# Two chained transformer layers on one core: the 16-bit turns move from TensorE to transposing transfers, and two copies move from ScalarE to VectorE

## The chip, the cores and the metric

The kernel runs on one core of a Trainium2 chip. A core has five engines that work side by side: TensorE (PE in the profile, with PEld for its weight loads), VectorE (DVE), ScalarE (ACT), GpSimd (POOL) and SyncE (SP), which here only issues transfers. Each runs its own list of instructions in order and waits on semaphores for the others; transfers are carried by 16 DMA engines. The metric is the time of one execution on the device in microseconds (us); less is better.

## The reference, cut to what matters

Two layers, each attention followed by a feed-forward part, over 2048 rows (2 batches of 1024) of 256 numbers. In the kernel the rows are 16 tiles of 128, numbered n = 0 to 15.

```python
# layer 0: x is (2, 1024, 256); 32 heads of 8, 8 key heads; causal
q, k, v = x @ Wq + bq, x @ Wk + bk, x @ Wv + bv      # then rotary on q and k
attn = softmax(where(kpos > qpos, -inf, q k^T / sqrt(8))) ; out = (attn @ v) @ Wo + bo
# feed-forward, operands cast to fp8
act = gelu(x8 @ w_gating[0]) * (x8 @ w_gating[1]) ; y = act8 @ w_linear
# layer 1: at each row, 16 heads of 16 attend to each other within the row
q, k = rope(x @ wq.T), rope(x @ wk.T) ; v = x @ wv.T
attn = softmax(einsum('bshd,bstd->bsht', q, k) / 4) @ v ; out = attn @ wo.T
# feed-forward with ternary weights: silu-gated hidden of 1024, RMS norm, projection to 256
```

The terms around these (layer norms, residual sums) are in both kernels alike.

## The kernel before

Every engine has a list of steps in ORDER, written out as words such as `qk.37`: the stage and its number. Each stage is a small function that waits on semaphores and issues its instructions; the list alone sets the order on an engine. A second pass exists for inputs out of range and is not run here. For layer 0 the score blocks ("quads", 144 in all, `qk`, `exp`, `mask`, `pv`) are the long thread through the lists; the other stages are strewn between them, several tiles ahead or behind.

TensorE wants its operand with the inner dimension on the partitions, so activations have to be turned (transposed) before a product. Four turns matter here:

- **Keys and queries of layer 0.** `qh` (ACT), `q0`, `kl` (DVE) and `ql` (POOL) write rows of fp16 pairs, high part and rest, into QX. `qxT` (PE, L639) turns them, 2 blocks of 128x128 for the keys and 8 for the queries of a tile, into PSUM; `kTc` (L1228) and `qTc` (L1235) on DVE copy them to kT and qT, which `qk` (L685) reads.
- **Normalized rows of layer 1.** `xn1` (DVE, f32) is turned by `xn1T` (PE, L590 and L591, f32), and `xn1Tc` (DVE, L1369 and L1371) makes the fp16 high part and the rest out of PSUM into xhs, for `qkv1` and `gu`.
- **Hidden activations of layer 1.** `ssq` (ACT, L1032) sums squares of the 1024 hidden values, `ssm` (DVE) and `rsg` (POOL) make the factor, `hxa` (ACT, L1037) writes the high part and `hx` (DVE, L1482) the rest, both fp16, into hx_b, of which there is one. `hxT` (PE, L876) turns 2 x 8 blocks, `hTc` (DVE, L1491) copies them to hT (one, too), and `dn1` (PE, L885) multiplies.
- **Queries and keys within a row (f32).** `gT` turns them on PE; `gTq` (DVE, L1422) and `gTk` (ACT, L1007) copy them out.

Results of PE other than scores and the attention sum go to three PSUM banks psA, psB and psC, which all fills share in the order of the list: a fill waits until the fill three before it has been emptied (EMPTIED). SP's list issues the transfers, in order: loads, the round trip of layer 1 through DRAM (`vw`, `vr` with three gathers L522, `ow`, `at1r`) and the output.

Of the kernel before, what the change touches and what calls it, by code (L numbers as in the profile page):

```python
# [1782 lines left out]
```

## Time and profile before

| what | value |
|---|---|
| three runs, median (least to most) | 600.06 us (599.37 to 602.33) |
| span of the profiled execution | 601.7 us |
| TensorE busy | 562.0 us, 93% |
| ScalarE busy | 469.6 us, 78% |
| VectorE busy | 426.6 us, 71% |
| GpSimd busy | 233.6 us, 39% |
| mean granted TensorE clock | 0.983 of full speed |

The span runs from the first to the last instruction of the one execution that was profiled; it is the only time of that execution that there is, and it is 0.3% above the median of the three runs. Busy time is the union of an engine's instructions. An engine that is nearly always busy in a stretch sets that stretch's length; one that is idle half of it can take more work there for nothing, if the work comes at the right moment.

### The profile page before, as it was taken

The numbers are of one execution on the slowest core, as the hardware profiler recorded it, in microseconds if no ns is written. First come the engines' busy times: TensorE is split into PE (matmuls) and PEld (weight loads), VectorE is DVE, ScalarE is ACT, GpSimd is POOL, SyncE is SP. The second block draws the span as 40 slices with busy tenths as digits, with TensorE's granted clock in tenths as the row PEclk, the third lists the DMA queues.
The fourth block names the chain that finished last, engine by engine and source line by source line (L and its number), as shares of the span: only waits on it lengthen the run. The fifth ranks groups of instructions, "written<-read, shape, count | busy, mean of one in ns | idle before, by whom it ended". The sixth has DMA issues, their size and how long they took to land. (4 is left out here: it accounts for less than half of the span.)

```text
span 601.7 us, 13300 instructions
## 1 busy us (share of the span) xinstructions
PE 562.0 (93%) x5153; PEld 290.7 (48%) x5153; DVE 426.6 (71%) x909; ACT 469.6 (78%) x607; POOL 233.6 (39%) x302
## 2 busy tenths in 40 slices
PE   3687898999999999999999999999999999999976
PEld 1332434433555555645544555565445454456654
DVE  5658889988789558856699877565555365658765
ACT  2378899999988997999878898777979877972631
POOL 3748666043533163306855641360232150250100
PEclk9778999999999999999999999999999999999989
DMA  8810101102041223030110330531301304035632
GB/s 265 303 36 2 36 1 35 36 2 49 6 62 33 33 59 39 27 37 3 19 17 2 64 54 27 89 55 27 54 10 36 45 20 69 17 68 85 94 57 48
DMA packets 150914, 30.40 MB, mean 51 GB/s; under 512 B 133952, under 2 KB 149568, under 8 KB 150848
## 3 DMA queue, kind: packets, MB, share of 16 engines
q1 hardware_dynamic: 150272, 29.19, 24.4%
q8 instruction: 42, 0.69, 0.5%
q10 hardware_dynamic: 576, 0.33, 0.3%
q14 instruction: 24, 0.20, 0.1%
HBM read 19.02 MB, written 10.49 MB: 49 GB/s over the span
## 5 line engine op out<-in xcount | busy, mean ns | idle before, releaser
L958 ACT ACTIVATE Pt<-psS 128x1024 f32<-128x1024 f32 x288 | 281.7, 1047 | 44.8 <-PE psS L685 25.9
L699 PE MATMUL psV<-Pt,vaug 128*32 128x512 f32 x1152 | 150.3, 611 | 0.3 <-POOL Pt L1645 0.3
L1645 POOL TENSOR_SCALAR_AFFINE_SELECT Pt<-Pt 128x1024 f32<-128x1024 f32 x64 | 71.7, 1145 | 43.8 <-ACT Pt L958 43.8
L685 PE MATMUL psS<-qTf,kTf 32*128 32x512 f16 x576 | 74.9, 390 | 7.3 <-ACT Pt L958 3.7
L685 PEld LDWEIGHTS psS<-qTf,kTf 32*128 32x128 f16 x576 | 20.3, 91 | 82.9 <-ACT Pt L958 48.1
L1695 POOL TENSOR_TENSOR ss<-ss,mhalf 128x1 f32<-128x1 f32 x16 | 9.5, 596 | 111.3 <-DVE ss L1476 111.3
L699 PEld LDWEIGHTS psV<-Pt,vaug 128*32 128x32 f32 x1152 | 25.7, 109 | 41.9 <-issue 35.9
L1016 ACT ACTIVATE stage<-psS 128x1024 f32<-128x1024 f32 x32 | 31.0, 1020 | 8.1 <-PE psS L821 7.9
L1686 POOL TENSOR_TENSOR r<-qk,cos 128x256 f32<-128x256 f32 x16 | 11.9, 744 | 63.9 <-ACT qk L991 58.0
L866 PE MATMUL psB<-wguT,xhs 128*128 128x512 bf16 x108 | 27.8, 380 | 0.0
L1032 ACT ACTIVATE qtmp<-qtmp 128x1024 bf16<-128x1024 f32 x16 | 16.9, 1059 | 12.9 <-PE psA L876 8.4
L1318 DVE SCALAR_TENSOR_TENSOR gw<-gw,gb 128x512 f32<-128x512 f32 x32 | 24.9, 781 | 2.5 <-ACT gw L973 2.5
L1327 DVE SCALAR_TENSOR_TENSOR ga<-gw,gb 128x512 bf16<-128x512 f32 x32 | 23.6, 738 | 3.9 <-ACT gw L984 3.8
L1636 POOL TENSOR_TENSOR QXf<-rt,QXf 128x512 f16<-128x512 f32 x16 | 19.1, 1195 | 18.1 <-ACT QXf L945 18.1
L1608 POOL TENSOR_SCALAR rs<-mv 128x1 f32<-128x1 f32 x16 | 5.3, 329 | 49.6 <-DVE mv L1164 49.6
L1625 POOL TENSOR_TENSOR rt<-qkv,cs 128x320 f32<-128x320 f32 x16 | 14.7, 916 | 24.5 <-DVE QXf L1220 15.8
L984 ACT ACTIVATE gw<-gw 128x512 f32<-128x512 f32 x32 | 21.2, 661 | 3.0 <-DVE gw L1318 2.9
L1482 DVE SCALAR_TENSOR_TENSOR qtmp<-qtmp,ss 128x1024 f16<-128x1024 f32 x16 | 21.4, 1336 | 2.9 <-ACT qtmp L1037 2.9
L866 PE MATMUL psC<-wguT,xhs 128*128 128x512 bf16 x88 | 22.8, 382 | 0.0
L973 ACT ACTIVATE gw<-gb 128x512 f32<-128x512 bf16 x32 | 21.2, 670 | 0.1
L885 PE MATMUL psA<-wpT,stmp 128*128 128x256 bf16 x176 | 21.1, 273 | 0.0
L1628 POOL TENSOR_TENSOR rt<-qkv,sn 128x160 f32<-128x160 f32 x32 | 20.9, 673 | 0.0
(381 smaller groups left out, 1246.5 us busy)
## 6 DMA issues: line engine op xcount, KB each, us to landing
qkvscr<-rqkv SPq DMA_DIRECT2D x16, 384.0 KB, 2.5
G<-qkvscr SPq DMA_DIRECT2D x24, 128.0 KB, 3.7
stage<-in_wg SPq DMA_DIRECT2D x4, 512.0 KB, 8.8
w8g<-qkvscr SPq DMA_DIRECT2D x16, 128.0 KB, 3.8
oscr<-o SPq DMA_DIRECT2D x16, 128.0 KB, 3.3
at<-oscr SPq DMA_DIRECT2D x16, 128.0 KB, 2.0
out<-yout SPq DMA_DIRECT2D x16, 128.0 KB, 2.5
x<-in_x SPq DMA_DIRECT2D x1, 1536.0 KB, 12.2
```

Of the source, the lines that this page charges most:

```text
L685: e.matmul(psS[j], kd[32 * j:32 * j + k, h, 128 * at:128 * at + 128], qd[32 * j:32 * j + k, 4 * h:4 * h + 4, :].rearrange("p s n -> p (s n ...
L699: ins = e.matmul(psV[32 * j:32 * j + 32, :], vaug[:, at, j, 32 * h:32 * h + 32], Pt[(4 * Q + j) % NP], start=(kb == 0 and h == 0), stop=(k ...
L866: ins = e.matmul(bank[:], src[:, pt, 128 * c:128 * c + 128], wguT[:, c, c0:c0 + 512], start=(k == 0), stop=(k == 3))
L885: ins = e.matmul(bank[:, 0:256], hT[:, pt, s, :], wpT[:, s, :], start=(k == 0), stop=(k == 15))
L958: e.activation(flat(Pt4[:, u % NP:u % NP + 2, :]), flat(psS4[:, j:j + 2, :]), ACT.Exp, scale=scale).then_inc(S["exp"], 1)
L973: e.activation(gw[:, half, :], gb[:, half, :], ACT.Square).then_inc(S["sq"], 1)
L984: e.activation(gw[:, half, :], gw[:, half, :], ACT.Tanh, scale=GC * GA).then_inc(S["th"], 1)
L1016: e.activation(P1[:, 4 * b:4 * b + 8, :].rearrange("p g n -> p (g n)"), flat(psS4[:, b:b + 2, :]), ACT.Exp, scale=SC1).then_inc(S["ex1"], 1)
L1318: e.scalar_tensor_tensor(gw[:, half, :], gw[:, half, :], 1.0 / GA, gb[:, half, :], ALU.add, ALU.mult).then_inc(S["ge1"], 1)
L1327: e.scalar_tensor_tensor(a, gw[:, half, :], 1.0, gg, ALU.add, ALU.mult).then_inc(S["ge3"], 1)
L1482: e.scalar_tensor_tensor(hx_b[:, 1, :], h1, sn[:, 2:3], hx_b[:, 0, :], ALU.mult, ALU.subtract).then_inc(S["hx"], 1)
L1645: e.affine_select(out=p, in_=p, pattern=[[0, 8], [1, 128]], compare_op=ALU.is_ge, fill=0.0, base=0, channel_multiplier=-1).then_inc(S["mas ...
```

## The change

Four new steps on SP replace the turns: `kt`, `qt`, `xt` and `ht` issue one transposing transfer each (DMA_TRANSPOSE, SBUF to SBUF), 64 in all: 128x256, 128x1024, 128x512 and 128x2048 numbers of 2 bytes per tile. `qxT`, `hxT` and, in the first pass, `xn1T` leave PE; `kTc`, `qTc`, `hTc` and the first pass of `xn1Tc` leave DVE. DVE gets `xs` (high part and rest of xn1, written to a new view xs_b), and takes `hxa` and `gTk` from ACT. The waits follow: `qk` now waits for d_kt and d_qt, `qkv1` and `gu` for d_xt, `dn1` for d_ht, and a writer of QX, xs_b or hx_b for the transfer that reads it. All five lists of ORDER are written anew; what stands at three places is shown below the diff.

```diff
+            def kt(n):
+                at = n % NT % RING
+                w.wait_ge("q0", n + 1)
+                w.wait_ge("kl", n + 1)
+                w.wait_ge("pv", keys_free(n))
+                e.dma_start_transpose(kT[:, :, 128 * at:128 * at + 128],
+                                      QX[n % len(QX)][:, 32:40, :].rearrange("p h c -> p (h c)")).then_inc(S[f"d_kt{n % 2}"], 16)
+            def qt(n):
+                w.wait_ge("qh", n + 1)
+                w.wait_ge("ql", n + 1)
+                if n >= len(qT):
+                    w.wait_ge("qk", 4 * QUAD_END[n - len(qT)])
+                e.dma_start_transpose(qT[n % len(qT)],
+                                      QX[n % len(QX)][:, 0:32, :].rearrange("p h c -> p (h c)")).then_inc(S[f"d_qt{n % 2}"], 16)
+            def xt(n):
+                dst = xhs[n % len(xhs)]
+                w.wait_ge("xs", 2 * n + 2)
+                w.wait_ge("qkv1", 2 * (n + 1 - len(xhs)))
+                w.wait_ge("gu", 4 * (n + 1 - len(xhs)))
+                e.dma_start_transpose(dst[:].rearrange("p a (c n) -> p (a c) n", n=128),
+                                      xs_b[n % len(xs_b)]).then_inc(S[f"d_xt{n % 2}"], 16)
+            def ht(n):
+                w.wait_ge("hxa", n + 1)
+                w.wait_ge("hx", n + 1)
+                w.wait_ge("dn1", n)
+                w.wait_ge("wsum", 2)
+                e.dma_start_transpose(hT.rearrange("p k s n -> p (k s) n"),
+                                      hx_b.rearrange("p k n -> p (k n)")).then_inc(S["d_ht"], 16)
...
-            def qxT(m):
...
-            def hxT(m):
...
             def dn1(n):
-                w.wait_ge("hTc", 2 * n + 2)
+                w.wait_ge("d_ht", 16 * (n + 1))
...
             def ssq(n):
                 w.wait_ge("hh", 2 * n + 2)
-                w.wait_ge("hxT", 2 * n)
+                w.wait_ge("d_ht", 16 * n)
...
-            def hxa(n):
-                w.wait_ge("rsg", n + 1)
-                e.activation(hx_b[:, 0, :], h1, ACT.Copy, scale=ss[n % len(ss)][:, 2:3]).then_inc(S["hxa"], 1)
...
+            def xs(n):
+                src, dst = xn1_b[n % len(xn1_b)], xs_b[n % len(xs_b)]
+                w.wait_ge("xn1", n + 1)
+                w.wait_ge(f"d_xt{n % 2}", 16 * (n // 2))
+                e.tensor_copy(dst[:, 0:256], src[:]).then_inc(S["xs"], 1)
+                w.wait_ge("xs", 2 * n + 1)
+                e.tensor_tensor(dst[:, 256:512], src[:], dst[:, 0:256], ALU.subtract).then_inc(S["xs"], 1)
...
+            def hxa(n):
+                w.wait_ge("rsg", n + 1)
+                w.wait_ge("ssq", n + 1)
+                w.wait_ge("d_ht", 16 * n)
+                e.tensor_scalar(hx_b[:, 0, :], h1, ss[n % len(ss)][:, 2:3], None, ALU.mult).then_inc(S["hxa"], 1)
```

The first place is SP's queue after the constants. `stage<-in_wg` and `r<-in_wgu` are weight loads of 512 KB. Before:

```order
L556 BRANCH_PREFETCH_HINT
L504 DMA r<-in_wgu 128x1024
L495 DMA stage<-in_wg 128x1024 x2
L498 DMA stage<-in_wl 128x4x256 x2
L504 DMA qk1T<-in_wgu 128x1024
L507 DMA r<-in_wp 128x4x256
```

After, with the keys' turn (kTf) and the queries' (qTf):

```order
L576 BRANCH_PREFETCH_HINT
L482 DMA stage<-in_wg 128x1024 x2
L532 DMA_TRANSPOSE kTf<-QXf 128x2x128
L540 DMA_TRANSPOSE qTf<-QXf 128x8x128
L485 DMA stage<-in_wl 128x4x256
L540 DMA_TRANSPOSE qTf<-QXf 128x8x128
L532 DMA_TRANSPOSE kTf<-QXf 128x2x128
L485 DMA stage<-in_wl 128x4x256
L491 DMA r<-in_wgu 128x1024
```

The first two turns now stand right behind two loads, and two later loads behind them.

The second place is PE up to the first scores (`psS<-qTf,kTf`). Before, L639 is the turn:

```order
L625 MATMUL psC<-wqkv,xnT 128x384
L626 MATMUL psC<-wqkv,xnT 128x384
L598 MATMUL psA<-qtmp,blockb 128x512
L639 MATMUL psB<-identh,QXf 128x128 x2
L639 MATMUL psC<-identh,QXf 128x128 x8
L685 MATMUL psS<-qTf,kTf 128x512 x4
```

After, where L743 is the feed-forward product `up` and L618 is `ts`:

```order
L646 MATMUL psA<-wqkv,xnT 128x384
L618 MATMUL psB<-qtmp,blockb 128x512
L743 MATMUL psC<-x8T,w8g 128x128 x8
L618 MATMUL psA<-qtmp,blockb 128x512
L743 MATMUL psB<-x8T,w8g 128x128 x8
L692 MATMUL psS<-qTf,kTf 128x512 x4
```

The ten turning matmuls are gone, and two `up` steps have come ahead of the first scores.

The third place is the end of PE's first pass, tiles 14 and 15. Before, L876 is `hxT` and L885 `dn1`:

```order
L841 MATMUL psA<-identf,o1r 128x128 x4
L876 MATMUL psB<-identh,qtmp 128x128 x8
L876 MATMUL psC<-identh,qtmp 128x128 x8
L885 MATMUL psA<-wpT,stmp 128x256 x16
L590 MATMUL psB<-identf,at_0 128x128
L853 MATMUL psC<-wo,at1T 128x256
L854 MATMUL psC<-wo,at1T 128x256
```

After, with L875 `gu`, L848 `o1T`, L885 `dn1` and L860 `wo1`:

```order
L875 MATMUL psA<-wguT,xhs 128x512 x4
L848 MATMUL psB<-identf,o1r 128x128 x4
L885 MATMUL psC<-wpT,stmp 128x256 x16
L860 MATMUL psA<-wo,at1T 128x256
L861 MATMUL psA<-wo,at1T 128x256
L610 MATMUL psB<-identf,at_0 128x128
```

Between the last products of a tile and its `dn1` nothing of PE is left that turns; `dn1` waits for the transfer itself.

## Rows read from the trace of the kernel before

**Rows 1.** The page, part 1: busy us (share of the span) xinstructions.

```profile
PE 562.0 (93%) x5153; PEld 290.7 (48%) x5153; DVE 426.6 (71%) x909; ACT 469.6 (78%) x607; POOL 233.6 (39%) x302
```

**Rows 2.** Busy time by stretches; columns are named in the first line.

```profile
core 0: us, PE busy (x) PEld busy (x) DVE busy (x) ACT busy (x) POOL busy (x), PEclk, DMA share, GB/s
...
20.00:150.00 130.00, 116.06 (x872) 48.90 (x872) 105.24 (x211) 114.88 (x153) 69.43 (x83) 0.93 0.14 43
150.00:550.00 400.00, 395.95 (x3818) 207.21 (x3818) 274.09 (x589) 334.22 (x428) 151.58 (x190) 1.00 0.24 39
550.00:602.00 52.00, 41.77 (x457) 30.87 (x449) 35.13 (x81) 16.56 (x22) 4.05 (x7) 0.97 0.39 67
```

**Rows 3.** The same stretches, line L639 (qxT) alone: PE, PEld.

```profile
20.00:150.00 130.00, 5.62 (x62) 3.97 (x62) 0.93 0.14 43
150.00:550.00 400.00, 8.34 (x98) 5.95 (x98) 1.00 0.24 39
```

**Rows 4.** The same stretches, line L876 (hxT) alone: PE, PEld.

```profile
150.00:550.00 400.00, 14.39 (x192) 11.72 (x192) 1.00 0.24 39
550.00:602.00 52.00, 4.54 (x64) 3.87 (x64) 0.97 0.39 67
```

**Rows 5.** Timeline at one xn1T: start us, us, instruction.

```profile
361.58 0.27 PE L590 MATMUL psC<-identf,xn 128*128 128x128 f32 x1
...
361.69 0.27 PE L591 MATMUL psC<-identf,xn 128*128 128x128 f32 x1
```

**Rows 6.** Groups of ACT: busy us, mean ns, idle before.

```profile
L1037 ACT ACTIVATE qtmp<-qtmp,ss 128x1024 f16<-128x1024 f32 x16 | 18.4, 1152 | 2.0 <-POOL ss L1695 1.9
...
L1007 ACT ACTIVATE qk1T<-psA 128x512 f32<-128x512 f32 x5 | 3.1, 611 | 2.8 <-PE psA L788 2.8
```

**Rows 7.** Groups of DVE, in the same columns.

```profile
L1482 DVE SCALAR_TENSOR_TENSOR qtmp<-qtmp,ss 128x1024 f16<-128x1024 f32 x16 | 21.4, 1336 | 2.9 <-ACT qtmp L1037 2.9
...
L1491 DVE COPY stmp<-psB 128x1024 f16<-128x1024 f16 x15 | 10.3, 688 | 11.2 <-PE psB L876 10.2 <-PE psA L885 1.0
...
L1104 DVE CAST w8g<-stage 128x1024 fp8e4<-128x1024 f32 x4 | 3.0, 758 | 3.9 <-DMA stage<-in_wg 3.9
...
L1422 DVE COPY kTf<-psA 128x512 f32<-128x512 f32 x4 | 2.7, 683 | 0.0
```

**Rows 8.** DMA issues: KB of each, median us from issue to landing.

```profile
G<-qkvscr SPq DMA_DIRECT2D x24, 128.0 KB, 3.7
stage<-in_wg SPq DMA_DIRECT2D x4, 512.0 KB, 8.8
...
at<-oscr SPq DMA_DIRECT2D x16, 128.0 KB, 2.0
...
stage<-in_wl SPq DMA_DIRECT2D x2, 512.0 KB, 3.8
```

**Rows 9.** DMA queue: packets, MB, share of 16 engines.

```profile
q1 hardware_dynamic: 150272, 29.19, 24.4%
```

**Rows 10.** Timeline from the last part of the first keys to the first exponentials.

```profile
20.05 0.28 DVE L1220 TENSOR_TENSOR QXf<-rt,QXf 128x128 f16<-128x128 f32 x1
...
21.36 0.69 DVE L1235 COPY qTf<-psC 128x1024 f16<-128x1024 f16 x1 [0.17 <-PE psC L639]
...
22.20 0.40 PE L685 MATMUL psS<-qTf,kTf 32*128 32x512 f16 x4 [0.88 <-DVE qTf L1235]
...
22.64 3.77 ACT L958 ACTIVATE Pt<-psS 128x1024 f32<-128x1024 f32 x4 [4.17 <-PE psS L685]
```

**Rows 11.** Timeline of SP's issues: three gathers.

```profile
196.21 3.40 SPq L522 DMA_DIRECT2D G<-qkvscr  x3
```

**Rows 12.** Timeline of tile 15's last links: ssq, hxa, hx, dn1.

```profile
586.91 1.06 ACT L1032 ACTIVATE qtmp<-qtmp 128x1024 bf16<-128x1024 f32 x1 [3.58 <-issue]
...
588.91 1.15 ACT L1037 ACTIVATE qtmp<-qtmp,ss 128x1024 f16<-128x1024 f32 x1 [0.85 <-POOL ss L1695]
...
590.73 1.27 DVE L1482 SCALAR_TENSOR_TENSOR qtmp<-qtmp,ss 128x1024 f16<-128x1024 f32 x1
...
596.01 1.92 PE L885 MATMUL psA<-wpT,stmp 128*128 128x256 bf16 x16
```

More of the change, by code:

```diff
@@ L215, in one_round @@
     steps = []
-    for word in (ROUND if n < NT else ROUND2)[engine].split():
+    for word in ROUND[engine].split():
         if word == "QUADS":
@@ L236 @@
     "xnT": lambda n: ("xnTc", 2 * n + 2), "qkv": lambda n: ("qkvc", n + 1),
[L237 removed]
+    "fxT": lambda m: ("fTc", m - 3 * NT + 1),
     "mT": lambda m: ("mTc", m - 2 * NT + 1), "obT": lambda n: ("att", 2 * n + 2), "attT": lambda n: ("attTc", n + 1),
     "wo0": lambda n: ("xa", n + 1), "up": lambda m: ("fh" if m % 2 else "g", m // 2 + 1), "down": lambda n: ("yff", n + 1), "flagT": lambda n: ("flag", 1), "wsum": lambda m: ("wmin", m + 1),
[L240 removed]
+    "xn1T": lambda n: ("xn1f", n - NT + 1), "qkv1": lambda m: ("v1c" if m % 2 else "qk1c", m // 2 + 1),
     "gT": lambda m: ("gTk" if m % 2 else "gTq", m // 2 + 1), "gTagain": lambda n: ("gTm", n - NT + 1),
@@ L265, in score_banks @@
     return dict(zip(fills[1:], fills))
-SEMS = """d_x0 d_x1 d_x2 d_id d_b d_cs d_w0 d_c d_w1 d_wg0 d_wg1 d_gu0 d_gu1 d_vw0 d_vw1 d_vr d_ow d_or d_out0 d_out1
-xnT qkv qxT fxT mT obT attT wo0 up down xn1T qkv1 gT S1m gTagain S1 PV1 o1T at1T wo1 gu hxT dn1 ts td tr qk pv rmm flagT
+SEMS = """d_ht d_kt0 d_kt1 d_qt0 d_qt1 d_xt0 d_xt1 d_x0 d_x1 d_x2 d_id d_b d_cs d_w0 d_c d_w1 d_wg0 d_wg1 d_gu0 d_gu1 d_vw0 d_vw1 d_vr d_ow d_or d_out0 d_out1
+xnT qkv fxT mT obT attT wo0 up down xn1T qkv1 gT S1m gTagain S1 PV1 o1T at1T wo1 gu dn1 ts td tr qk pv rmm flagT
 qh exp g sq fh th qk1c gTk ex1 tg ssq hxa tc tde sin
-idc vz tab cst w8 w8m w8s tsc tm tcs tw ln0 xn xnTc qkvc va wide q0 kl kTc qTc fTc rmax rcomb mxn mTc ob att attTc xa ge1 ge3 ge3b a8c yff
-wh wsq wsum ln1 xn1 xn1Tc xn1f wl wmin v1c ro1 ro2 gTq m1 gTm o1r o1 sg hh ssm hx hTc at1Tc yo yout osum flag rng rngb
+idc vz tab cst w8 w8m w8s tsc tm tcs tw ln0 xn xnTc qkvc va wide q0 kl xs fTc rmax rcomb mxn mTc ob att attTc xa ge1 ge3 ge3b a8c yff
+wh wsq wsum ln1 xn1 xn1Tc xn1f wl wmin v1c ro1 ro2 gTq m1 gTm o1r o1 sg hh ssm hx at1Tc yo yout osum flag rng rngb
 zero gz zf rs0 rope ql mask ge4 xf rs1 ro1p rsg w8a""".split()
@@ L387, in build @@
         xhs = several(2, "xhs", [128, 2, 256], F16)
+        xs_b = [flat(b[:]).bitcast(F16) for b in xn1T_b]
         qk1 = several(1, "qk1", [128, 512])
@@ L546, in all_landed @@
                 w.wait_ge("d_or", 16 * NT * passes)
-            run = {"wg": wg, "wt": wt, "vw": vw, "vr": vr, "ow": ow, "at1r": at1r, "out": out}
+                w.wait_ge("d_ht", 16 * NT * passes)
+            run = {"wg": wg, "wt": wt, "vw": vw, "vr": vr, "ow": ow, "at1r": at1r, "out": out, "kt": kt, "qt": qt, "xt": xt, "ht": ht}
             load_first()
@@ L626, in qkv @@
                 e.matmul(bank[:, 0:384], src[:, 1, :], wqkv[:, 1, :], start=False, stop=True).then_inc(S["qkv"], 1)
-            def qxT(m):
-                n, part = divmod(m, 2)
-                src = QX[n % len(QX)]
-                w.wait_ge("idc", 2)
-                w.wait_ge("q0", n + 1)
-                w.wait_ge("kl", n + 1)
-                if part == 1:
-                    w.wait_ge("qh", n + 1)
-                    w.wait_ge("ql", n + 1)
-                bank = shared("qxT", m)[:].bitcast(F16).rearrange("p (s n) -> p s n", n=128)
-                for at, u in enumerate(range(8) if part else range(8, 10)):
-                    ins = e.transpose(bank[:, at, :], src[:, 4 * u:4 * u + 4, :].rearrange("p r c -> p (r c)"), identh[:])
-                ins.then_inc(S["qxT"], 1)
             def transpose_heads(bank, units, sem):
@@ L769, in qkv1 @@
                     src = xhs[n % len(xhs)]
-                    w.wait_ge("xn1Tc", 2 * n + 2)
+                    w.wait_ge(f"d_xt{n % 2}", 16 * (n // 2 + 1))
                     w.wait_ge("wh", 1)
@@ L859, in gu @@
                 src = xhs[n % len(xhs)]
-                w.wait_ge("xn1Tc", 2 * n + 2)
+                if n < NT:
+                    w.wait_ge(f"d_xt{n % 2}", 16 * (n // 2 + 1))
+                w.wait_ge("xn1Tc", 2 * (n + 1 - NT))
                 w.wait_ge("tw", 8)
@@ L868, in gu @@
                 ins.then_inc(S["gu"], 1)
-            def hxT(m):
-                n, pt = divmod(m, 2)
-                w.wait_ge("hx" if pt else "hxa", n + 1)
-                w.wait_ge("idc", 2)
-                bank = shared("hxT", m)[:].bitcast(F16).rearrange("p (s n) -> p s n", n=128)
-                for s in range(8):
-                    ins = e.transpose(bank[:, s, :], hx_b[:, pt, 128 * s:128 * s + 128], identh[:])
-                ins.then_inc(S["hxT"], 1)
             def dn1(n):
-                w.wait_ge("hTc", 2 * n + 2)
+                w.wait_ge("d_ht", 16 * (n + 1))
                 w.wait_ge("tw", 12)
@@ L1033, in ssq @@
                              accum_out=ss[n % len(ss)][:, 0:1]).then_inc(S["ssq"], 1)
-            def hxa(n):
-                w.wait_ge("rsg", n + 1)
-                e.activation(hx_b[:, 0, :], h1, ACT.Copy, scale=ss[n % len(ss)][:, 2:3]).then_inc(S["hxa"], 1)
-            run = {"wh": wh, "wsq": wsq, "qh": qh, "g": g, "hxa": hxa, "sin": sin, "tc": tc, "tde": tde, "exp": exp, "sq": sq, "fh": fh, "th": th, "qk1c": qk1c, "gTk": gTk, "ex1": ex1,
+            run = {"wh": wh, "wsq": wsq, "qh": qh, "g": g, "sin": sin, "tc": tc, "tde": tde, "exp": exp, "sq": sq, "fh": fh, "th": th, "qk1c": qk1c, "ex1": ex1,
                    "tg": tg, "ssq": ssq}
@@ L1365, in xn1Tc @@
                 dst = xhs[n % len(xhs)]
-                w.wait_ge("xn1T", n + 1)
-                w.wait_ge("qkv1", min(2 * (n + 1 - len(xhs)), 2 * NT))
+                w.wait_ge("xn1T", n - NT + 1)
+                w.wait_ge("qkv1", 2 * NT)
                 w.wait_ge("gu", 4 * (n + 1 - len(xhs)))
                 e.tensor_copy(dst[:, 0, :], bank[:, 0:256]).then_inc(S["xn1Tc"], 1)
-                w.wait_ge("xn1Tc", 2 * n + 1)
+                w.wait_ge("xn1Tc", 2 * (n - NT) + 1)
                 e.tensor_tensor(dst[:, 1, :], bank[:, 0:256], dst[:, 0, :], ALU.subtract).then_inc(S["xn1Tc"], 1)
-                if n >= NT:
-                    w.wait_ge("qkv1", 2 * (n + 1 - len(xn1T_b)))
-                    e.tensor_copy(flat(xn1T_b[n % len(xn1T_b)][:]), bank[:, 0:256]).then_inc(S["xn1f"], 1)
+                w.wait_ge("qkv1", 2 * (n + 1 - len(xn1T_b)))
+                e.tensor_copy(flat(xn1T_b[n % len(xn1T_b)][:]), bank[:, 0:256]).then_inc(S["xn1f"], 1)
             def wl(n):
@@ L1422, in gTq, with gTk @@
                 e.tensor_copy(turned(n, 0).rearrange("p j n -> p (j n)"), bank[:]).then_inc(S["gTq"], 1)
+            def gTk(n):
+                w.wait_ge("tc", 12)
+                w.wait_ge("gT", 2 * n + 2)
+                w.wait_ge("S1", 4 * (n - 1) if n < NT else 4 * n)
+                bank = psM[filled["gT", 2 * n + 1] % len(psM)]
+                e.tensor_copy(turned(n, 1).rearrange("p j n -> p (j n)"), bank[:]).then_inc(S["gTk"], 1)
             def m1(n):
@@ L1584, in zf @@
             def zf(n):
-                w.wait_ge("qxT", 2 * NT)
+                for p in range(2):
+                    w.wait_ge(f"d_qt{p}", 8 * NT)
+                    w.wait_ge(f"d_kt{p}", 8 * NT)
                 e.memset(QXf[:], 0.0).then_inc(S["zf"], 1)
```

61 lines of the change are left out of this document (17 added, 44 removed), and 268 rows, old and new, of tables (ORDER, ROUND).

## The prediction

> **What bounds the kernel now.** I read part 1 of the page first: TensorE is busy 562.0 us of 601.7, the next engine, ScalarE, 469.6 [rows 1]. A mean over a run of several stages says little, so the second view is busy time by stretches [rows 2]. In the 400 us from 150 to 550 TensorE is busy 395.95 us, 99%, and ScalarE 334.22, 84%: there TensorE alone sets the pace, and what is taken off it shortens the stretch. From 20 to 150 us TensorE has 116.06 of 130 and ScalarE 114.88, so both are near the limit and neither alone decides. After 550 us nothing is full (41.77 of 52): a chain of waits sets the length, and there latency counts.
>
> **What TensorE loses.** The turns of keys and queries hold it 5.62 us from 20 to 150 and 8.34 us from 150 to 550 [rows 3]; those of the hidden activations 14.39 us in the packed stretch and 4.54 us at the end [rows 4]. A pair of xn1T takes from 361.58 to 361.96, 0.38 us [rows 5]; 13 of the 16 lie in the packed stretch (4.9 us), two before it (0.8), one after (0.4). So the packed stretch sheds 8.34 + 14.39 + 4.9 = 27.6 us, the early one 6.4, the end 4.9; together 39 of 562. I count the 27.6 in full. Of the early 6.4 I count 3, because ScalarE loses nothing there (its two moved steps begin only with layer 1) and is as full as TensorE. Of the end's 4.9 I count 2, because the chain there waits for data.
>
> **What the vector engines do.** ScalarE sheds 16 hxa of 1.152 us and 16 gTk of 0.611: 28 us [rows 6]. That leaves 441 us of about 573, 77%, its present share, so it stays second. VectorE sheds 48 copies of 1024 columns at 0.688, 33 us, and the small copies of keys and of xhs. It gains 16 gTk at 0.683, 11 us, and 16 hxa, which no row shows on it: the nearest are a cast of as many columns, 0.758, and the two-input hx, 1.336 [rows 7]. I take 1.0, between them, 16 us, with 12 and 21 as its bounds. xs (two passes over 256 columns) replaces the two of xn1Tc and I set it equal. VectorE so ends at or under its 426.6 us, with at least 140 us free; the cover holds, and its work costs nothing. If hxa stood uncovered on the last chain it would cost nothing either, since it replaces 1.15 us of ScalarE there. Fewer fills of the three shared banks (80 fewer) remove waits that I do not price.
>
> **What the transfers cost.** No row shows a transposing transfer. Bounds for the largest, ht with 512 KB: below, the plain 512 KB load, 3.8 us from issue to landing; above, four times the 128 KB gather in 64-byte pieces, 4 x 3.7 = 14.8 us [rows 8]. I take 5 us, near the plain load, because source and destination rows are long on one side at least and nothing goes to DRAM and back; scaled alike, qt (256 KB) has 3 us, xt and kt about 2, the plain 128 KB transfer's 2.0 [rows 8]. The Trainium skill, DMA: Bandwidth & Descriptors, section on latency and other measured facts, gives 261 GB/s for a transposing transfer; by an estimate from that page ht would move its data in 2.0 us, and the forecast would be about a microsecond shorter. No run here shows that rate.
>
> Where these land on a path:
>
> - **Start.** Now the last part of the first keys ends at 20.33 and the first scores start at 22.20, 1.9 us later [rows 10]. After the change, kt.0 and qt.0 stand on SP behind two 512 KB loads. Landing then costs between 2.0 us (nothing ahead) and 8.8 us (what such a load takes in this phase) [rows 8], so the first scores move by 0 to 7 us. I take 4; two up steps fill TensorE meanwhile, but ScalarE's exponentials start later.
> - **Middle.** Turns are issued tiles ahead, and the hidden activations' loop is not tight: a tile comes about every 28 us (16 tiles in 450 us), and the loop of one hx_b is ssq to the end of hx, 586.91 to 592.00, 5.1 us [rows 12], plus ht. 5.1 + 5 fits nearly three times. I put 0.
> - **End.** Four tiles, 12 to 15, go through that loop in the last 50 us, 12.5 us each, so ht up to 7.4 us is hidden between them. Behind the last hx (ends 592.00) dn1 now starts at 596.01, 4.0 us later [rows 12]; ht at 5 us adds 1.
>
> Sum, against the profiled span: 601.7 - 27.6 - 3 - 2 + 4 + 1 = 574.1. Its median run stands to its span as 600.06 to 601.7, so the forecast is **573 us**. Its own range is 560 to 583: all 39 us shed and nothing added gives 562.7, or 561 on the median's scale; the upper starting cost with nothing won early or at the end gives 582.1, or 580.5.
>
> **Rival 1: the turns are cheap but late.** All turns now go through one queue that SP serves in order, 152 steps. Three gathers alone hold it 3.40 us [rows 11], and a step that waits for a late tile holds every turn behind it, and behind the turns qk, qkv1, gu and dn1 on TensorE. For it: TensorE has 4 us of slack in 400, so each wait shows. Against it: turns have been placed with work between them and their users. If each tile loses 1 us of TensorE this way, 16 us, the time is 589; range 583 to 600. Chance 0.20.
>
> **Rival 2, slower than before: the turns move in small pieces.** If a turn costs what the gather costs per byte, ht takes 14.8 us. Each of the last four tiles then exceeds its 12.5 us by 5.1 + 14.8 - 12.5 = 7.4, 30 us, and the last link adds 9.8 in place of 1. The time is 573 + 30 + 9 = 612. The point from which the sign turns: the gain of 27 us is eaten by four tiles at 7 us each, that is at ht of about 14 us. The queue would be nearly full too: 960 KB of turns a tile are 7.5 x 3.7 = 28 us, 444 in all, beside the 24.4% of 601.7 us, 147, that its transfers have now [rows 9]; so 612 to 640. For it: every transfer of this kernel that scatters small pieces is slow for its size. Against it: the pieces here are SBUF to SBUF. Chance 0.20.
>
> **Rival 3, slower too: block after block.** A tile needs 2 + 8 + 4 + 16 = 30 blocks of 128x128, 480 in all. If the blocks go one after another, the price of one decides: a quarter of the plain 128 KB transfer is 0.5 us, a transfer for each is 2.0 [rows 8]. From 480 x 1.19 = 573 on, the queue alone is the kernel. At the middle, 1.25 us, it is 600 us, and 747 with the 147 us that the queue carries already. Chance 0.10, because the plain rows give no sign of such a limit. The Trainium skill, VectorE: DVE Perf Modes, section The three transpose paths, speaks against the change: it gives 1309 ns for a 128x128 block by a transfer and 390 ns on TensorE. If that were the price of each in a row, an estimate from that page is 628 us for the 480. No run here shows it; on TensorE the trace has 192 blocks in 14.39 us, 75 ns each [rows 4], where the page has 390.
>
> **How the numbers follow.** The forecast has 0.50, rival 1 0.20, rival 2 0.20, rival 3 0.10. A measurement of this kernel tells about 0.5% from no change, 597 to 603 us. Under 597 lie the forecast and 0.14 of rival 1: 0.64 faster. Within lie the rest of rival 1 and a little of rival 2, 0.08. The rest, 0.28, is slower. The range is 558 to 628: below, the forecast's own edge; above, so far into rival 2 that what is left out, rival 3, the top of rival 2 and a sliver below, is 2 in 10.
>
> **What the profile would show.** If I am right: TensorE busy near 523 us and again 98% or more in the middle; the ht transfers landing within 7 us of issue; dn1 at the end starting within 6 us of hx. Rival 1 would show TensorE idle in the middle ahead of L692, waiting for kTf or qTf, with short landings. Rival 2 would show ht landing after 12 us or more and the DMA share over 60%. Rival 3 would show the DMA transfers nearly without a gap and TensorE under 80%. A granted clock under full speed in the middle, which is 1.00 now [rows 2], would upset the sum as well: more gaps in TensorE's work could bring it, and I have put nothing in for that.

## The result and the profile after

The changed kernel takes 576.97 us (median of 4 runs, 575.09 to 578.89) where the kernel before takes 599.73 (4 runs, 599.37 to 602.33): a ratio of 0.962, with a 95% interval of 0.958 to 0.966. The forecast was 573 us. The profiled execution of the changed kernel is the fastest of the four, 575.09 us, with a span of 573.3. That of the kernel before has a span of 601.7 us and is above its median. So the two profiles differ by 28.4 us, the medians by 22.8, and 5.6 us of what the profiles show belong to these two executions alone.

Part 1 and the clock line of part 2 of the page of the changed kernel, and its busy time by stretches; they answer to [rows 1] and [rows 2]:

```profile
PE 517.7 (90%) x4657; PEld 255.0 (44%) x4705; DVE 415.1 (72%) x877; ACT 445.7 (78%) x575; POOL 235.8 (41%) x302
...
PEclk9999999999999999999999999999999999999999
```

```profile
core 0: us, PE busy (x) PEld busy (x) DVE busy (x) ACT busy (x) POOL busy (x), PEclk, DMA share, GB/s
...
20.00:150.00 130.00, 109.06 (x801) 43.62 (x812) 105.23 (x213) 116.03 (x153) 70.07 (x84) 1.00 0.24 60
150.00:525.00 375.00, 366.58 (x3451) 183.94 (x3483) 267.72 (x566) 314.02 (x402) 152.35 (x188) 1.00 0.41 71
```

In the middle TensorE seems 97.8% busy (366.58 of 375). That is a gap in the records, not in the work. Busy time of the first product of `gu` alone, in the middle stretch, after (L875) and before (L866), PE and PEld:

```profile
150.00:525.00 375.00, 46.90 (x179) 17.90 (x212) 1.00 0.41 71
```

```profile
150.00:550.00 400.00, 53.99 (x212) 18.64 (x212) 1.00 0.24 39
```

The 212 weight loads are there in both, but 33 matmuls are missing after, 7.1 us. With them the middle is 373.7 of 375: TensorE is still full there. From 20 to 150 us its idle time grew, 20.9 us against 13.9; about 11 records are missing there (801 matmuls beside 812 weight loads), so some 4 us of the 20.9 are not idle. The granted clock of that stretch was 1.00, the upper of its two levels throughout, against 0.93 before, so the two busy times are not at one clock.

The length can be split at the last exponential, since the attention of layer 0 ends there and the packed stretch with it. Groups of the exponentials (L958 in both), before and then after; the last two times of the row are the first and last start:

```profile
L958 ACT ACTIVATE Pt<-psS x288: 1003/1025/1296, 22.6 to 534.1; 128x1024 f32<-128x1024 f32 x144
```

```profile
L958 ACT ACTIVATE Pt<-psS x288: 1004/1023/1099, 30.8 to 507.5; 128x1024 f32<-128x1024 f32 x144
```

The first starts 8.2 us later, the last 26.6 us earlier, and from there to the end of the span it is 65.8 us instead of 67.6. The late start doesn't last. Busy time and count of the exponentials up to 60 and up to 150 us, before and then after:

```profile
0.00:60.00 60.00, 18.98 (x20) 0.86 0.46 152
...
0.00:150.00 150.00, 71.24 (x71) 0.94 0.24 76
```

```profile
0.00:60.00 60.00, 18.44 (x20) 1.00 0.53 168
...
0.00:150.00 150.00, 69.85 (x72) 1.00 0.33 92
```

At 60 us the changed kernel has begun as many as the kernel before, at 150 us one more. So the first 150 us gave and cost about nothing, the stretch from there to the last exponential gave 26.6 us, and the end 1.8. All engines in that stretch, before and then after:

```profile
150.00:534.10 384.10, 380.06 (x3619) 197.46 (x3620) 259.62 (x558) 324.35 (x415) 145.71 (x183) 1.00 0.23 37
```

```profile
150.00:507.50 357.50, 350.52 (x3272) 173.04 (x3305) 254.87 (x541) 307.40 (x394) 146.57 (x180) 1.00 0.41 72
```

TensorE was idle 4.0 us of it before and, with the missing records (some 7 us), next to nothing after; its own work there fell by about 22 us. Without its turns it has as many weight loads before, some 3304, as after, 3305, so as much other work stands in the stretch. That also bounds what the new lists can have gained there by better places alone: about the 4.0 us that were idle.

The transfers, which no row of before could show: issue on SP and landing (min, median, max) of `kt`, `qt`, `xt` and `ht`, from the views of L532, L540, L548 and L556:

```profile
L532 SPq DMA_TRANSPOSE kTf<-QXf x16: 1170/1298/1982, 25.5 to 475.4; - x16
...
DMA to landing us min/median/max: 2.3/2.7/4.0
```

```profile
L540 SPq DMA_TRANSPOSE qTf<-QXf x16: 1231/1244/2302, 26.9 to 457.1; - x16
...
  PE psS L692: 1.3, 1
...
DMA to landing us min/median/max: 3.0/3.2/4.9
```

```profile
DMA to landing us min/median/max: 2.4/2.5/4.4
```

```profile
L556 SPq DMA_TRANSPOSE stmp<-qtmp x16: 1328/1642/2646, 166.8 to 564.4; - x16
...
  PEld psC L885: 2.7, 1
...
DMA to landing us min/median/max: 3.7/3.8/4.9
```

512 KB land in 3.8 us, and in the whole run the matmuls wait for a turn for a few microseconds only. What is new is the price of an issue: 1.2 to 1.6 us of SP's queue for a transposing transfer (medians), where the plain stores and loads of the round trip take 0.33 to 0.38 (L501, L514, L520) and a gather about 1.0 (L509).

The end of tile 15, in the timeline, answers to [rows 12]:

```profile
562.22 0.75 DVE L1472 TENSOR_SCALAR qtmp<-qtmp,ss 128x1024 f16<-128x1024 f32 x1
...
563.01 1.28 DVE L1478 SCALAR_TENSOR_TENSOR qtmp<-qtmp,ss 128x1024 f16<-128x1024 f32 x1
...
564.36 1.70 SPq L556 DMA_TRANSPOSE stmp<-qtmp  x1
...
568.12 1.92 PE L885 MATMUL psA<-wpT,stmp 128*128 128x256 bf16 x16 [0.18 <-DMA stmp<-qtmp]
```

`dn1` starts 3.8 us after `hx` ends; with turns on TensorE it was 4.0. And the start, which answers to [rows 10]:

```profile
24.16 0.69 DVE L1093 CAST w8g<-stage 128x1024 fp8e4<-128x1024 f32 x1 [6.22 <-DMA stage<-in_wg]
25.13 0.29 DVE L1209 TENSOR_TENSOR QXf<-rt,QXf 128x128 f16<-128x128 f32 x1
25.51 1.29 SPq L532 DMA_TRANSPOSE kTf<-QXf  x1
...
26.91 1.23 SPq L540 DMA_TRANSPOSE qTf<-QXf  x1
...
30.16 0.62 PE L692 MATMUL psS<-qTf,kTf 32*128 32x512 f16 x4 [1.30 <-DMA qTf<-QXf]
```

The first scores come at 30.16 against 22.20. About 5 us of the 8 are there before any transfer is issued: VectorE's list now has the cast `w8.2` ahead of `kl.0`, and the cast waits for weights.

### The profile page after: what moved, and what is told of

It is laid out like the page before. It is cut to its first block, busy times and chain, and to the rows that moved or that the text cites. A ratio compares the mean times of both kernels' runs of the same rounds, so it can differ in the third digit from the quotient of the medians.

```text
span 573.3 us, 12407 instructions
## 1 busy us (share of the span) xinstructions
PE 517.7 (90%) x4657; PEld 255.0 (44%) x4705; DVE 415.1 (72%) x877; ACT 445.7 (78%) x575; POOL 235.8 (41%) x302
## 4 chain that ended last, share of the span: by engine, by line
PE 63%; DMA 7%; DVE 4%; issue 3%; ACT 3%; SPq 2%; DVEq 0%; ACTq 0%
PE psV L706 18%; PE psS L692 7%; PE psC L875 3%; PE psS L828 2%; PE psA L875 2%; PE psB L782 2%; PE psB L885 2%; PE psB L875 2%; DMA G<-qkvscr 2%; DMA qkvscr<-rqkv 2%; ACT Pt L958 2%; PE psB L743 1%; SPq L509 1%; PE psA L782 1%; DMA oscr<-o 1%
## 5 line engine op out<-in xcount | busy, mean ns | idle before, releaser
L958 ACT ACTIVATE Pt<-psS 128x1024 f32<-128x1024 f32 x288 | 279.4, 1028 | 42.2 <-PE psS L692 36.3
L706 PE MATMUL psV<-Pt,vaug 128*32 128x512 f32 x1152 | 152.3, 606 | 1.9 <-DVE ob L1265 1.9
L1635 POOL TENSOR_SCALAR_AFFINE_SELECT Pt<-Pt 128x1024 f32<-128x1024 f32 x64 | 74.7, 1192 | 55.4 <-ACT Pt L958 55.4
L692 PE MATMUL psS<-qTf,kTf 32*128 32x512 f16 x576 | 64.7, 389 | 3.5 <-ACT Pt L958 2.2
L692 PEld LDWEIGHTS psS<-qTf,kTf 32*128 32x128 f16 x576 | 17.3, 91 | 79.1 <-ACT Pt L958 43.7
L1009 ACT ACTIVATE stage<-psS 128x1024 f32<-128x1024 f32 x32 | 31.0, 1022 | 18.6 <-PE psS L828 18.5
L706 PEld LDWEIGHTS psV<-Pt,vaug 128*32 128x32 f32 x1152 | 24.0, 108 | 40.0 <-issue 32.0
L1676 POOL TENSOR_TENSOR r<-qk,cos 128x256 f32<-128x256 f32 x16 | 13.1, 816 | 47.2 <-ACT qk L991 40.6
L1302 DVE SCALAR_TENSOR_TENSOR ga<-gw,gb 128x512 bf16<-128x512 f32 x32 | 23.9, 746 | 6.7 <-ACT gw L984 6.7
L1025 ACT ACTIVATE qtmp<-qtmp 128x1024 bf16<-128x1024 f32 x16 | 17.0, 1060 | 14.4 <-issue 11.8
L1626 POOL TENSOR_TENSOR QXf<-rt,QXf 128x512 f16<-128x512 f32 x16 | 18.6, 1165 | 19.0 <-ACT QXf L945 19.0
L875 PE MATMUL psC<-wguT,xhs 128*128 128x512 bf16 x74 | 19.9, 380 | 2.5 <-issue 1.9
L875 PE MATMUL psB<-wguT,xhs 128*128 128x512 bf16 x74 | 19.5, 380 | 2.5 <-DVE stmp L1451 1.1
L1618 POOL TENSOR_TENSOR rt<-qkv,sn 128x160 f32<-128x160 f32 x32 | 20.9, 671 | 0.0
L945 ACT ACTIVATE QXf<-rt 128x512 f16<-128x512 f32 x16 | 10.3, 641 | 12.6 <-POOL rt L1621 12.6
```

Source lines behind the costliest of these rows:

```text
L692: e.matmul(psS[j], kd[32 * j:32 * j + k, h, 128 * at:128 * at + 128], qd[32 * j:32 * j + k, 4 * h:4 * h + 4, :].rearrange("p s n -> p (s n ...
L706: ins = e.matmul(psV[32 * j:32 * j + 32, :], vaug[:, at, j, 32 * h:32 * h + 32], Pt[(4 * Q + j) % NP], start=(kb == 0 and h == 0), stop=(k ...
L875: ins = e.matmul(bank[:], src[:, pt, 128 * c:128 * c + 128], wguT[:, c, c0:c0 + 512], start=(k == 0), stop=(k == 3))
L958: e.activation(flat(Pt4[:, u % NP:u % NP + 2, :]), flat(psS4[:, j:j + 2, :]), ACT.Exp, scale=scale).then_inc(S["exp"], 1)
L1009: e.activation(P1[:, 4 * b:4 * b + 8, :].rearrange("p g n -> p (g n)"), flat(psS4[:, b:b + 2, :]), ACT.Exp, scale=SC1).then_inc(S["ex1"], 1)
L1302: e.scalar_tensor_tensor(a, gw[:, half, :], 1.0, gg, ALU.add, ALU.mult).then_inc(S["ge3"], 1)
```

## The experiments

Two theories were to be told apart at first. **Theory 1**: the gain is TensorE's own work, which left the full stretch; the transfers' latency is hidden; who makes the two copies matters little. **The rivals**: relief of ScalarE gained it; or the lists, which were rewritten whole, did; or the latency still costs and something else pays for it. Each comparison is with the kernel before, run beside it on the same chip (medians 600.1 to 600.9 us), or with the changed kernel's 577.0.

### What TensorE's work is worth

**b_hxt_twice**, the kernel before with dead work: every turn of hx is made twice.

```diff
-                for s in range(8):
+                for s in list(range(8)) * 2:
                     ins = e.transpose(bank[:, s, :], hx_b[:, pt, 128 * s:128 * s + 128], identh[:])
```

> The kernel before with dead work added: each hxT makes its eight turns twice into the same bank, 256 more turns on PE, nothing else. The added work is 256 turns at 56 to 75 ns, 14.4 to 19.2 us. Theory 1 (TensorE's own work sets the time): 600 + 12 to 19 = 612 to 619 us. Rival C (TensorE is not the bound, what was gained came from VectorE and ScalarE): 600 to 604.

Measured: 609.57 us, ratio 1.015 (1.013 to 1.018), 8.6 us more. Busy time of L876 in this run:

```profile
150.00:550.00 400.00, 25.11 (x384) 22.43 (x384) 1.00 0.23 37
550.00:620.00 70.00, 7.96 (x128) 7.43 (x128) 0.98 0.35 58
```

Against [rows 4], 10.7 and 3.4 us were added, 14.1 in all, for 8.6 us of time: 0.6 us for each.

**a_dead_turns**, the changed kernel with 256 turns that nothing reads, at the head of `dn1`.

```diff
             def dn1(n):
...
+                    for k in range(16):
+                        e.transpose(dead[:, 4 + k % 4, :], hT[:, k // 8, k % 8, :], identh[:])
```

> The changed kernel with dead work added: at the head of each dn1, 16 turns of hT on PE into a part of dn1's bank that nothing reads; transfers, order and other engines are left as they are. 256 turns at 56 to 75 ns, 14.4 to 19.2 us. Theory 1: 577 + 12 to 19 = 589 to 596 us, so about what the h turns' share of the gain was. Rival C: 577 to 581.

Measured: 587.81 us, ratio to before 0.976 (0.974 to 0.979), against the changed kernel 10.8 us more by the medians and 8.6 by the two ratios. The added line, L887:

```profile
150.00:525.00 375.00, 11.69 (x176) 10.13 (x176) 1.00 0.39 68
525.00:590.00 65.00, 6.93 (x80) 6.19 (x80) 0.94 0.61 103
```

18.6 us added for 9 to 11 of time, 0.5 to 0.6. So TensorE's work is on the path in both kernels, and the rival by which it isn't falls. Both came out under the forecast of 12 to 19. The price of a microsecond is less sure than that. In the profiled execution of a_dead_turns, which is the slowest of its four (591.47 us), the stretch from 150 us to the last exponential is 10.1 us longer for 11.7 added, and what follows 6.3 longer for 6.9: 0.9. In that of b_hxt_twice, the fastest of its four, the last exponential starts 4.9 us later for 10.7 added.

### One part alone, in the old lists

**b_ht_dma**: the kernel before, where only the turns of hx are a transfer. `ht` stands on SP's queue where `hx` comes in VectorE's list.

```diff
+            def ht(n):
+                w.wait_ge("hxa", n + 1); w.wait_ge("hx", n + 1); w.wait_ge("dn1", n)
+                e.dma_start_transpose(...).then_inc(S["d_ht"], 16)
-   pe: hxT.*     dve: hTc.*
+   sp: ... vw.8 at1r.5 ht.6 vr.8 ow.6 ...
```

> The kernel before with one part of the change alone: the turns of hx by one transposing transfer per tile (ht), in place of 256 turns on PE and 32 evictions on VectorE. Both copies stay on ScalarE, and qxT and xn1T stay on PE. The order of before is kept; ht stands on SP's queue where its source is ready. Theory 1 (the time came from work taken off TensorE in the packed stretch, the landing is hidden): L876 took 14.39 us between 150 and 550 us and the windows after it little, so 600 - 14 to 18 = 582 to 586 us, less whatever dn1 waits for ht in an order that was not made for it: at most some 2 us for each of 16 tiles, which would give 586 to 600. Rival A (the landing costs as much as the turns did): 598 or more, with PE idle ahead of dn1 by 1 us or more a tile. Rival B (the gain comes from the new lists of the order): 597 to 603, with PE's busy time 14 us lower and its idle time 14 us higher, spread over many lines.

Measured: 635.74 us, ratio 1.060 (1.056 to 1.064), 35 us slower, although TensorE has 14 to 19 us less to do. SP's queue around `ht.6`, and what the matmuls waited for most (us in total, times, longest):

```profile
401.40 1.59 SPq L536 DMA_TRANSPOSE stmp<-qtmp  x1
403.08 2.95 SPq L513 DMA_DIRECT2D G<-qkvscr  x3
```

```profile
PE psA L788 <- DMA G<-qkvscr: 9.1, 2, 6.4
PE psB L590 <- DMA at<-oscr: 7.6, 1, 7.6
...
PE psB L788 <- DMA G<-qkvscr: 6.7, 1, 6.7
```

The issue before it ends at 391.67 us, so `ht.6` stood at the head of the queue for 9.7 us, because hT was still in use until `dn1.5`, and the gathers behind it came late, and TensorE with them. The largest wait for an `ht` itself (L885) was 1.8 us. That is the forecast's rival 1, the one queue, in full size.

**b_ht_dma2** is the same but for the places of `ht` on SP: each stands where, by the trace of before, its source and the free hT were both there.

> The same part alone as in b_ht_dma (the turns of hx by one transfer per tile in the kernel before, everything else as before), but ht stands on SP's queue at the time at which its source and the free hT were both there in the trace of before, so that far fewer stores and loads (ow, at1r, vw, vr) wait behind it. In b_ht_dma the queue spent 118 us waiting for a dn1 at the head of ht, and the run was 35 us slower than before. Theory 1' (the transfer itself costs little, its place in the one queue decides): most of the 35 us goes, 590 to 606 us; the end still waits, since dn1.14, dn1.15 and their ht stand in a row there and nothing covers a landing of 3.7 us. Rival (the landing itself, or its bandwidth, is what costs): 625 us or more, as b_ht_dma.

Measured: 614.22 us, ratio 1.023 (1.020 to 1.025). 21.5 of the 35 us were the places in one queue. What is left is slower than the kernel before by 13.5 us (9.4 between the two profiles), more than theory 1' had, and it is all behind the last exponential. That starts at 526.5 us, 7.6 earlier than in the kernel before, so the packed stretch did gain from the turns; but from there to the end it is 84.6 us, not 67.6. There ScalarE stood 19.0 us in front of `ssq` in two waits for `ht`, since `ssq(n)` writes hx_b, which `ht(n-1)` still has to read, and that waits for `dn1(n-2)`. One hx_b and one hT, with a transfer between, tie three tiles together; a turn through PSUM did not.

```profile
ACT qtmp L1032 <- DMA stmp<-qtmp: 19.0, 2, 10.4
```

**b_copies_dve**: the kernel before, where only the two copies go to VectorE, `hxa` just ahead of `hx` and `gTk` up to 13 places behind `gTq`.

> The kernel before with only the two copies moved: hxa just ahead of hx on VectorE and gTk some places behind gTq on VectorE, not on ScalarE. All turns stay on PE. Theory 1: the copies cost ScalarE 17 us and VectorE some 24 us, both engines have idle time in the middle, so 600 +- 4 us. Rival C (relief of ScalarE is what gained): 590 or less. Rival D (VectorE gets too full beside its evictions): 605 or more.

Measured: 613.91 us, ratio 1.024 (1.020 to 1.029), 13 us slower: the time that rival D gave, but its reason isn't shown. VectorE was busy 448.2 us, 21.6 more, yet from 150 us to the last exponential that is 274.29 of 385.9 us, 71%. The profiled execution is the fastest of the four, 8.3 us over the kernel before: the last exponential starts at 535.9, 1.8 us later, and what follows takes 74.1 us instead of 67.6. So most of the loss is in the end, where `hxa` and `hx` now follow each other on VectorE. Whether it is the engine or the places that cost here was not varied, and in the changed kernel places were most of it, as a_copies_act2 shows below.

So each of these two parts alone, in the old lists, makes the kernel slower, and together with the rest they make it faster.

### The copies in the changed kernel

**a_copies_act** puts them back on ScalarE, `hxa` mostly two places behind `ssq`, `gTk` right behind its turn.

> The changed kernel with only the two copies put back on ScalarE: hxa behind ssq (2 places, more where its rsg comes later) and gTk behind its gT. Turns stay transfers. Theory 1 (the copies are neither here nor there): 577 +- 3 us. Since moving them alone cost the kernel before 13 us (b_copies_dve, VectorE still had 32 evictions of turns and 22 us of copies more), a rival says that they cost the changed kernel as well: 565 to 572 us. A second rival says that ScalarE's relief gained: 582 or more.

Measured: 611.20 us, ratio to before 1.018 (1.016 to 1.021), 34 us above the changed kernel. ScalarE's waits tell that this is in part the places that I chose:

```profile
ACT Pt L956 <- PE psS L690: 31.4, 51, 2.3
ACT qtmp L1028 <- POOL ss L1681: 16.7, 9, 4.4
```

**a_copies_act2** has the same work in better places: each copy stands in ScalarE's list at the time at which its source was ready in the trace of the changed kernel.

> The changed kernel with the two copies back on ScalarE as in a_copies_act, but each stands in ScalarE's list at the time at which its source was ready in the trace of the changed kernel, not two places behind ssq: in a_copies_act ScalarE stood 16.7 us in front of hxa waiting for GpSimd's rsg, 10.1 us in front of gTk, and 31.4 us for scores, and the run took 611 us. Theory 1 (who makes the copies is worth little, what cost 34 us was the place in the list): 577 to 585 us, with the waits in front of hxa and gTk under 6 us together. Rival (ScalarE's 23 us more of work are on the path, since it is the second fullest engine and feeds VectorE and TensorE): 595 or more although these waits are gone.

Measured: 586.58 us, ratio to before 0.979 (0.976 to 0.982), 9.6 us above the changed kernel; the intervals are apart. The wait in front of `hxa` is gone, but the last exponential starts at 514.5, not 507.5. Of the 34 us, 25 were places and about 10 are the work: it is worth something that ScalarE doesn't do it. Theory 1, by which the copies were neither here nor there, falls at this point, and neither bound of the rival (595 or more) was met. The waits in front of `gTk` were 15 us, above the 6 that the expectation set, so even the 10 may still hold some cost of places. Where the 10 lie is seen in the stretch from 150 us to the last exponential, which is 7.0 us longer than in the changed kernel; the rest, 3.1 us, is behind it:

```profile
150.00:514.50 364.50, 353.89 (x3270) 174.28 (x3304) 238.47 (x517) 323.02 (x418) 144.97 (x180) 1.00 0.40 70
```

With the 34 matmuls whose records are missing, TensorE has some 3 us of idle time there again. This run is also the nearest that there is to the turns and the new lists without the copies: 14.3 us faster than the kernel before.

### How much room the turns have

**a_ht_twice**: each `ht` is issued again after it has landed, into the same place.

```diff
+                for again in range(2):
+                    if again:
+                        w.wait_ge("d_ht", 32 * n + 16)
```

> The changed kernel with each ht issued twice, the second after the first has landed, so that hT is there about 5.4 us later (3.8 us of landing and 1.6 us of issue) and SP's queue stands still for as long; what is computed is the same. Theory 1 (the landing is hidden in the middle, not at the end): the last four tiles pay up to 5.4 us each, less 3 us of slack, and a few stores and loads behind ht come late: 577 + 5 to 20 = 582 to 597 us. Rival (the landing is on the path of every tile): 16 x 5.4 = 86 us more, 660.

Measured: 612.87 us, ratio to before 1.019 (1.016 to 1.021), 36 us above the changed kernel: far over theory 1, far under the 86 of the rival. SP stood 35.5 us in the 16 waits for the first landing, 2.2 each, so with the second issue a turn came 3.8 us later (my 5.4 counted the issue twice). The last exponential starts at 527.2 us, 19.7 later than in the changed kernel, and what follows takes 84.9 us, 19.1 more: half of the loss is in the middle and half in the end.

**a_ht_twice_free** adds a tile of its own for the squares of `ssq`, which nobody reads, so that `ssq` waits for no transfer; **a_ssq_free** has only that tile, without the second `ht`.

```diff
             def ssq(n):
-                w.wait_ge("d_ht", 16 * n)
-                e.activation(hx_b[:, 0, :].bitcast(BF16), h1, ACT.Square, ...)
+                e.activation(sqj[:], h1, ACT.Square, ...)       # 128x1024, fp8
```

> a_ht_twice (each ht in series twice) with the same tile for ssq's squares. In a_ht_twice, 36 us slower than the changed kernel, ScalarE stood 35.0 us in front of ssq, where the changed kernel has 11.8. Theory (a late ht costs mainly by way of ScalarE, whose list stands still in front of ssq): 15 to 30 us of the 36 come back, 583 to 597 us. Rival (it costs by way of SP's one queue, which stands 35.5 us in ht waiting for the first landing, with the loads and stores behind it): 605 to 613, ssq's waits gone and others in their place.

Measured: 602.96 us, ratio to before 1.005 (1.002 to 1.007). 10 of the 36 us came back, between the two expectations. The 35.0 us in front of `ssq` are gone, but ScalarE waits elsewhere instead. What ScalarE waited for in a_ht_twice, then in a_ht_twice_free:

```profile
ACT Pt L961 <- PE psS L695: 43.1, 55, 6.0
ACT qtmp L1028 <- issue: 35.0, 8, 11.1
ACT stage L1012 <- PE psS L831: 17.4, 11, 7.9
```

```profile
ACT Pt L962 <- PE psS L696: 46.5, 59, 7.0
ACT stage L1013 <- PE psS L832: 29.7, 13, 13.3
```

So about a quarter of what a late `ht` costs goes by way of `ssq`. The rest fits what stands behind it on SP, but no run separated the queue from the landing here.

> The changed kernel with one wait less: ScalarE's ssq(n) writes its squares, which nobody reads, over the first half of hx_b, and so waits for ht(n-1), which waits for dn1(n-2). Here the squares go to a tile of their own (8 bits wide, the sum is the same), and ssq waits for no transfer; the copies still do. In the changed kernel ScalarE stood in front of ssq for 6.1 us at 528.6 and 5.7 us at 551.8, both near the end, and at no other tile. Theory: ssq.13 and ssq.14 come up to 5 us sooner, hx.14 then waits only for the landing (550.9) and not for ssq, ssm and rsg behind it, so the end is 2 to 5 us shorter: 572 to 575 us. Rival (another wait ends there as late, dn1.13's own): 576 to 578.

Measured: 578.39 us, ratio to before 0.964 (0.961 to 0.967): no gain. The two waits in front of `ssq` near the end, 11.8 us, cost nothing in the changed kernel.

### The start

**a_start** moves `w8.2` behind `kl.0` on VectorE and `qk.0` ahead of `up.0` on TensorE; **a_start2** also moves `exp.0` ahead of `g.0` on ScalarE.

> The changed kernel with two steps moved at the start alone: VectorE's w8.2, which waits 6.2 us for a load of in_wg until 24.16, stands behind kl.0, not ahead of it, and PE's qk.0 stands ahead of up.0. kl.0 can then run at about 20, its transfer land at 24, and the first scores come at some 25.5 us, 4.6 us sooner than the 30.16 of the changed kernel. Theory 1'' (most of the 8 us by which the first scores are late is the order of the list, not the transfer): the first scores at 24.5 to 26.5, and the time lower by what ScalarE, the fullest engine up to 150 us, keeps of it: 572 to 576. Rival (the transfers cause the late start): first scores still at 29 or later, time as before at 577.

> As a_start, and exp.0 stands ahead of g.0 in ScalarE's list. In a_start the first scores came at 26.84 us, 3.3 us sooner than the 30.16 of the changed kernel, but the first exponential only at 30.14 (30.81 in the changed kernel), since ScalarE's list has g.0 and qh.1 ahead of it and g.0 waits for the first up step; the time stayed at 577.5. Theory (the start is on the path, and ScalarE's list held it back): the first exponential at 27.5 to 28, and 2 to 3 us of it reach the end: 573.5 to 575.5 us. Rival (nothing of the first 30 us is on the path up to 150 us by more than a microsecond: the scores and exponentials catch up later, since up, g and fh wait in their place): 576 to 578.5.

The start of a_start2 in its timeline:

```profile
19.40 1.30 SPq L530 DMA_TRANSPOSE kTf<-QXf  x1
20.80 2.28 SPq L538 DMA_TRANSPOSE qTf<-QXf  x1
...
27.35 0.61 PE L690 MATMUL psS<-qTf,kTf 32*128 32x512 f16 x4 [5.75 <-DMA qTf<-QXf]
...
28.00 1.94 ACT L956 ACTIVATE Pt<-psS 128x1024 f32<-128x1024 f32 x2 [3.03 <-PE psS L690]
```

The list was half of the delay only: `kt.0` is issued 6.1 us sooner, the scores come 2.8 us sooner, since `qt.0` now lands 6.5 us after its issue, amid the weight loads, not 3.2 (a_start: 26.84). In time: a_start 577.47 us, ratio to before 0.962 (0.960 to 0.965), nothing; a_start2 575.21, 0.959 (0.956 to 0.962), 1.8 us less than the changed kernel. The intervals of the two overlap, and the trace doesn't show a gain either: although the first exponential starts 2.8 us sooner, 20 exponentials have begun by 60 us and 72 by 150 us, as in the changed kernel, and the span is 573.6 us against 573.3. The profiled execution had a granted clock of 0.62 from 15 to 30 us and 0.70 from 30 to 45, where the changed kernel's had 1.00, so it is not a clean comparison. That fits the rival: the scores and exponentials catch up.

## Why the prediction was right, and where its steps were not

The direction and the size were right, 573 against 577. By steps:

- **"There TensorE alone sets the pace": right, with a condition.** It is full in the middle before and after, and more work on it makes either kernel longer. Between the two profiles the middle gave 26.6 us, where I counted 27.6 "in full"; in all TensorE is busy 517.7 us, 525 to 530 with the 48 matmuls whose records are missing, where I had 523. But the turns alone didn't give them: with the copies back on ScalarE (a_copies_act2) it is 7.0 us less, which leaves 19.6 for the turns and the lists. The dead turns point the same way. At 0.5 to 0.6 us of time per microsecond, the price by the medians, the 39 us shed are worth 20 to 23, not the 32.6 that I counted. Adding is not removing, and the profiled pair of a_dead_turns gives 0.9, so this price is an estimate.
- **The copies: a term was missing.** I wrote that ScalarE "stays second" and VectorE's "work costs nothing". The second held in the changed kernel: VectorE is busy 415.1 us, and `hxa` takes 0.75 us on it, under my 1.0. That it held because 33 us of evictions left it is not shown; the same copies cost the kernel before 13 us (b_copies_dve), mostly in the end. The first missed that ScalarE, at 84% in the middle, was near enough to the bound for about 10 us (a_copies_act2), although it shed only 24 us, not 28. This missing gain and the turns counted too high have about cancelled: that 573 came so near is in part luck.
- **Landings: right in size.** 5, 3, 2 and 2 us were assumed for `ht`, `qt`, `xt` and `kt`; 3.8, 3.2, 2.5 and 2.7 came. Rivals 2 and 3 needed 14 us, or 1.19 us for each block; `ht` has 16 blocks in 3.8 us. They fall, and with them the reading of the page by which a transfer is slower: the Trainium skill, VectorE: DVE Perf Modes, section The three transpose paths, has 1309 ns against 390 for a 128x128 block; here it is 0.24 us per block in a transfer of 16, and 56 to 75 ns on TensorE. So TensorE turns a block faster in this trace too, but the time of a transfer isn't TensorE's. No run here has a transfer of one block; the smallest, `kt` with two, takes 2.7 us to land.
- **Start: mis-sized.** +4 was forecast for the first scores and +8.0 measured, over the bound of 7. I looked at the two loads ahead on SP, not at VectorE's list, which put a 6.2 us wait for weights ahead of the keys. What it cost the whole is next to nothing: by 60 us as many exponentials have begun as before, and a kernel with the first scores 2.8 us sooner isn't shown to be faster (a_start2). With the 3 us counted for the early turns that makes +1 for the first 150 us, and about 0 measured.
- **Middle: right number, wrong reason.** I put 0, because the loop of hx_b fits nearly three times into a tile's 28 us. a_ht_twice refutes the reason: 3.8 us more in that loop cost 36 us, and between the profiles 19.7 of the 38.8 us lie before the last exponential. The room in the loop is not the room in the lists. `ht` waits for `dn1(n-1)`, `ssq(n+1)` for `ht`, and gathers and stores stand behind `ht` on SP.
- **End: +1 forecast for the last link, 0 measured** (3.8 us from `hx` to `dn1` against 4.0); with the 2 us counted for its turns the end should have gained 1, and gained 1.8. The reserve was overrated here too: I had up to 7.4 us of `ht` hidden between the last tiles, and in a_ht_twice, where the two issues and landings take about 7.6, the end lost 19.1 us.
- **Rival 1** had its mechanism right and its chance is hard to judge. It did not appear in the changed kernel, but in b_ht_dma it cost 21.5 us, with nothing different but the places of 16 issues.

What stays open: how the gain divides. By the medians the turns with the new lists gave 14.3 us (a_copies_act2) and moving the copies 9.6 more, 23.9 together, where the changed kernel's own comparison has 22.8. The 9.6 are an upper bound, since a_copies_act2 may not have the best places. The new lists themselves were not separated from the turns; in the middle they can have given about 4.0 us at most, the time in which TensorE was idle before. The lists of the changed kernel with all turns on TensorE, which would show it, were not tried.

## What to carry to other kernels

Where lists are written out by hand, a part tried alone in the old lists says little about the change: two parts of a change that gained 23 us were losses of 35 and 13 us by themselves, and the same instructions in better places on the same engine gave back 21 and 25 us. Before moving a step to a queue that others use, look at what each step there waits for, above all a buffer that is single: the price is what stands behind it. And before you count a bound engine's microseconds in full, double some of its work, and ask whether the second fullest engine can follow: here part of the gain came only because ScalarE was relieved too.
